# The first layer's router on rows that are not yet normalized

## What is computed

```
h = h + _L0_attn_ref(_layernorm(h, axis=-1), Wq, Wk, Wv, ...)
h = h + _L0_ffn_ref(_layernorm(h, axis=-1), expert_sel, keys, values)

def _L0_ffn_ref(x, expert_sel, keys, values):
    sel = jax.nn.sigmoid(xt @ expert_sel.T)
    sel_val, sel_idx = jax.lax.top_k(sel, TOP_K)          # TOP_K = 2 of E = 32
    w = zeros((T, E)).at[arange(T)[:, None], sel_idx].add(sel_val)
    h = jax.nn.relu(einsum('td,edh->teh', xt, keys))
    out = einsum('teh,te,ehv->tv', h, w, values)
```

## Time and profile before

| | us |
|---|---|
| median of 3 executions | 1150.5 |
| lowest, highest | 1148.85, 1151.22 |
| span of the profiled execution (first to last instruction) | 1146.4 |
| PE busy in the span | 936.4 (82%) |
| DVE busy | 876.0 (76%) |
| POOL busy | 673.3 (59%) |
| ACT busy | 511.0 (45%) |

### The profile page before, as it was taken

One profiled execution on the slowest core, in us unless ns is written; L12 is line 12 of the kernel. 1 busy time (PEld: TensorE's weight loads), 2 busy tenths in 40 slices (PEclk: granted clock), 3 DMA queues, 4 the chain that ended last, 5 costly groups with the idle time before them and its releaser, 6 DMA issues.

```text
span 1146.4 us, 21968 instructions
## 1 busy us (share of the span) xinstructions
PE 936.4 (82%) x6140; PEld 789.8 (69%) x6140; DVE 876.0 (76%) x3376; ACT 511.0 (45%) x1358; POOL 673.3 (59%) x622
## 2 busy tenths in 40 slices
PE   6999999999999973476667876566638999999992
PEld 2666676777667663466556765565638999999992
DVE  0588988988898966466678897677866888888883
ACT  1355555445555421111113545555524666656651
POOL 1036667666666633667777577766674545555552
PEclk9999999999999975678897887777759999999996
DMA  9856655666664032487789854455356888889886
GB/s 374 349 181 223 215 192 199 234 219 215 206 230 142 26 85 71 129 220 208 208 245 329 258 166 152 161 178 181 102 197 233 257 259 272 283 268 342 274 300 223
DMA packets 118667, 246.60 MB, mean 215 GB/s; under 512 B 20914, under 2 KB 85936, under 8 KB 112400
## 3 DMA queue, kind: packets, MB, share of 16 engines
q1 hardware_dynamic: 78016, 191.53, 50.6%
q0 software_dynamic: 18592, 34.68, 8.9%
q10 hardware_dynamic: 21936, 18.98, 5.5%
HBM read 201.68 MB, written 45.43 MB: 216 GB/s over the span
## 4 chain that ended last, share of the span: by engine, by line
PE 43%; DVE 22%; DMA 10%; issue 9%; SPq 7%; ACT 5%; POOL 3%; ACTq 1%; DVEq 0%; POOLq 0%
PE ps L950 11%; PE ps L931 9%; PE ps L734 4%; DMA x_hi<-results_L 3%; PE ps L801 3%; PE ps L785 3%; POOL lists_L L2061 2%; SPq L597 2%; SPq L599 2%; SPq L590 2%; DMA x_lo<-results_L 2%; PE ps L727 2%; PE ps L910 2%; PE ps L773 2%; PE ps L751 2%
## 5 line engine op out<-in xcount | busy, mean ns | idle before, releaser
L2061 POOL DMA_INDIRECT lists_L<-rows,slots x250 | 281.0, 1124 | 185.0 <-issue 173.1
L2089 POOL DMA_INDIRECT results_L<-xin x145 | 144.0, 993 | 122.7 <-DVE xin L1861 95.0
L2089 POOL DMA_INDIRECT results_L<-xin,place x146 | 143.8, 985 | 64.3 <-issue 39.5
L734 PE MATMUL ps<-xin,w_emb 128*128 128x512 f32 x292 | 138.2, 610 | 9.7 <-DMA w_emb<-in_w_main 8.6
L950 PE MATMUL ps<-xin,QK 128*128 128x128 f32 x838 | 115.3, 288 | 6.5 <-DVE QK L1813 4.4
L950 PEld LDWEIGHTS ps<-xin,QK 128*128 128x128 f32 x838 | 107.0, 203 | 8.0 <-DVE QK L1813 4.7
L931 PE MATMUL ps<-x_hi,x_lo 128*128 128x256 f32 (+1 forms) x324 | 98.5, 304 | 1.1 <-DVE x_lo L1829 1.1
L910 PE MATMUL ps<-ident,xin 128*128 128x128 f32 x291 | 65.9, 309 | 39.6 <-DMA xin<-lists_L 37.4
L2070 POOL TENSOR_TENSOR x_lo<-xin,x_hi 128x2048 fp32r<-128x2048 f32 x13 | 60.1, 4625 | 63.8 <-ACT x_hi L1118 63.5
L1271 ACT ACTIVATE QK<-ps,xin 128x256 f32<-128x256 f32 x164 | 64.4, 475 | 71.5 <-PE ps L931 71.5
L734 PEld LDWEIGHTS ps<-xin,w_emb 128*128 128x128 f32 x292 | 52.8, 194 | 59.2 <-issue 48.6
(11 more groups left out here) (310 smaller groups left out, 2443.1 us busy)
## 6 DMA issues: line engine op xcount, KB each, us to landing
xin<-in_x_main SPq DMA_DIRECT2D x48, 1536.0 KB, 6.8
xin<-in_w_L SPq DMA_DIRECT2D x81, 578.0 KB
xin<-in_w_L SPq DMA_DIRECT2D x98, 128.0 KB
xin<-lists_L SPq DMA_DIRECT2D x64, 132.0 KB
xin<-in_w_L ACTq DMA_DIRECT2D x65, 128.0 KB
xin<-in_difference SPq DMA_DIRECT2D x13, 640.0 KB
xin<-in_distance SPq DMA_DIRECT2D x13, 640.0 KB
x_hi<-results_L SPq DMA_DIRECT2D x11, 640.0 KB, 5.9
```

The source lines that it names most:

```text
L734: mm = pe.matmul(psE[h], w_emb[:, k, :], xin[h][c][:, n, :], start=(k == 0), stop=False, skip_group_check=True)
L2061: pool.indirect_dma_start(out=lists[l.name], out_offset=bass.IndirectOffsetOnAxis(ap=slots_of(l, g, h)[:, t, k:k + 1], axis=0), in_=buf[:, ...
L2089: pool.indirect_dma_start(out=results[l.name], out_offset=bass.IndirectOffsetOnAxis(ap=where, axis=0), in_=yblk[u][:, q, :], in_offset=Non ...
```

## The change

Only the first layer's routing is changed.

- The five transposes of the normalized rows on PE and ACT's copy of them are gone. The router multiplies `h1T` itself, which has its features along the partitions already, right after `b2`'s transposes of it, by `centered`: the router's matrix less each column's mean over the features. That matrix is made once at the start, by one product with ones (`sel_sums`) and one DVE instruction.
- The logits lie in the second pair of PSUM banks now. DVE copies them in `r2`, which is called right after the statistics of the group's rows, ahead of `a1_apply` (that makes `ntok`). The rest of the old `r2`, from the two largest on, is `r2_top` and stays where it was.
- The logits now lack the factor 1/sqrt(var + eps). A new DVE instruction, `scaled`, multiplies the two largest by it. ACT's exponential takes that product. `scaled` stands behind `r2_top`, directly ahead of `r2_gate`.
- In the last step (no attention left) DVE finds the two largest and the masks first, then refines the root and normalizes the rows, then makes the slots, and last the gates.
- Waits are added on PE for the logits' copy (ahead of the next product into the second pair) and for `htok`'s copy (ahead of the next product into the third pair).

The core of the diff. PE, the router's product (`r2`) and its place in `step`:

```diff
             def r2(l, g, h, j):
                 s = S[l.name]
-                pe.wait_ge(s.x2T_ready, g + 1)
+                if l is L1:
+                    pe.wait_ge(s.x2T_ready, g + 1)
+                else:
+                    pe.wait_ge(h1T_ready, g + 1)
+                    pe.wait_ge(consts_dve, 2)
                 for t in range(TILES):
-                    mm = pe.matmul(pair[2][0:l.rows, t * l.E:(t + 1) * l.E], x2T[l.name][:, t, :], selT[l.name][:, :],
-                                   start=True, stop=True)
+                    of_tile = x2T[:, t, :] if l is L1 else h1T[:, t * ROWS:(t + 1) * ROWS]
+                    mm = pe.matmul(logits[l.name][:, t * l.E:(t + 1) * l.E], of_tile,
+                                   selT["L1"] if l is L1 else centered[:, :], start=True, stop=True)
...
                 b2(g, h, j)
+                r2(L0, g, h, j)
                 tiles(4, 9)
...
                 if ahead_a:
                     a3(g + 1, o, jo)
-                r1(L0, g, h, j)
-                if ahead_a:
                     a4(g + 1, o, jo)
-                r2(L0, g, h, j)
```

ACT, the exponential (`r2`) and `front_step`:

```diff
                 if l is L0:
-                    act.activation(w.eg[:, :, :], w.top8[:, :, 0:TOP], ACT.Exp, scale=-1.0).then_inc(s.eg_ready, 1)
+                    act.activation(w.eg[:, :, :], w.eg[:, :, :], ACT.Exp, scale=-1.0).then_inc(s.eg_ready, 1)
...
                     a3(g + 1, o, jo)
-                r1_x2T(L0, g, h, j)
                 r1_rows1(L0, g, h, j)
```

DVE, the new function and `front_step`:

```diff
+            def scaled(g):
+                w = W["L0"]
+                dve.tensor_tensor(w.eg[:, :, :], w.top8[:, :, 0:TOP], LNB.rs[:, :, None].to_broadcast([ROWS, TILES, TOP]),
+                                  ALU.mult).then_inc(S["L0"].top_ready, 1)
...
                 r1(L0, g, h, j)
-                if ahead_a:
-                    a1_apply(g + 1, o, jo)
+                r2(L0, g, h, j)
+                if not ahead_a:
+                    st = r2_top(L0, g, h, j)
+                    r1_apply(L0, g, h, j)
+                    scaled(g)
+                    r3(L0, g, h, j, st)
+                    r3_slots(L0, g, h, j, st)
+                    r2_gate(L0, g, h, j, st)
+                    return
+                a1_apply(g + 1, o, jo)
                 r1_apply(L0, g, h, j)
...
-                st = r2(L0, g, h, j)
+                st = r2_top(L0, g, h, j)
+                scaled(g)
                 r2_gate(L0, g, h, j, st)
```

More of the change, by code:

```diff
@@ L291, in build @@
         pair = [ps[:, 2 + 2 * n:4 + 2 * n, :].rearrange("p b n -> p (b n)") for n in range(3)]
+        routed = {l.name: pair[2][0:l.rows, 0:TILES * l.E] for l in (L0, L1)}
+        logits = {"L0": pair[1][0:L0.rows, 0:TILES * L0.E], "L1": routed["L1"]}
+        sel_sums = pair[2][:, 2 * BANK - L0.E:]
         ident = sb("ident", [128, 128])
@@ L1477, in newton @@
                 dve.wait_ge(step, st.all())
-            NA, NBB, NR = 6, 1, {"L0": 11, "L1": 14}
+            NA, NBB = 6, 1
+            routing_steps = {l.name: Steps(0) for l in (L0, L1)}
             def e0(g, h, j):
@@ L1562, in r2 @@
                 s = S[l.name]
-                st = Steps(NR[l.name] * g + 3)
+                st = routing_steps[l.name]
                 E, w, p = l.E, W[l.name], l.rows
                 dve.wait_ge(s.lg_ps, g + 1)
-                logit = pair[2][0:p, 0:TILES * E].rearrange("p (t e) -> p t e", t=TILES)
+                logit = logits[l.name].rearrange("p (t e) -> p t e", t=TILES)
                 if l is L0:
-                    dve.tensor_copy(w.lg[:, :, 0:E], logit).then_inc(s.dveR, st.one())
+                    dve.tensor_copy(w.lg[:, :, 0:E], logit).then_inc(s.lg_read, 1)
                 else:
@@ L1571, in r2, with r2_top @@
                                                 rb_rows[:, None, :].to_broadcast([p, TILES, E]), ALU.add).then_inc(s.dveR, st.one())
-                dve.wait_ge(s.dveR, st.all())
+            def r2_top(l, g, h, j):
+                s = S[l.name]
+                st = routing_steps[l.name]
+                E, w, p = l.E, W[l.name], l.rows
+                if l is L0:
+                    dve.wait_ge(s.lg_read, g + 1)
+                else:
+                    dve.wait_ge(s.dveR, st.all())
                 dve.wait_ge(s.eg_ready, g)
@@ L1576, in r2 @@
                     ins = dve.max(w.top8[:, t, :], w.lg[:, t, 0:E])
-                if l is L0:
-                    ins.then_inc(s.top_ready, 1)
-                    dve.wait_ge(s.top_ready, g + 1)
-                else:
-                    ins.then_inc(s.dveR, st.one())
-                    dve.wait_ge(s.dveR, st.all())
+                ins.then_inc(s.dveR, st.one())
+                dve.wait_ge(s.dveR, st.all())
                 if l is L1:
@@ L1964, in chosen_first @@
             def chosen_first(g):
-                counts[g] = r2(L1, g, g % 2, g // 2)
+                r2(L1, g, g % 2, g // 2)
+                counts[g] = r2_top(L1, g, g % 2, g // 2)
             def slots_then(g):
```

47 lines of the change are left out of this document (27 added, 20 removed).

## The result

| | before | after |
|---|---|---|
| median of 11 executions on the same chip, us | 1148.9 | 1158.2 |
| span of the profiled execution, us | 1146.4 | 1154.1 |
| steps 2 to 11 of the front stage, pick to pick, us | 25.29 to 25.45 | 25.96 to 26.65 |
| PE busy in these ten steps, us | 248.5 of 253.4 | 249.3 of 263.5 |

The ratio is 1.0079 with a 95% interval of 1.0062 to 1.0097: 9.1 us slower, where 3.1 were forecast. The sign and the loop were right; the size was not. 1158.2 is just outside the range as it was written, 1148.0 to 1158.0. Counted from the kernel before it is further out: the range was set from a median of 1150.5 of three executions, so its upper end is 7.5 us slower, against the measured 9.1.

A forecast was written before the change was run, and what follows sets the result against it. The prediction took a loop through DVE's `x_lo`, POOL's held issue and `x_lo0`, and DVE's `oh` to bound the steps. Terms 8.8 - 0.5 - 0.7 - 4.5 = +3.1 us took 1150.5 to 1153.6 us, range 1148.0 to 1158.0.

The forecast's parts named there:

- What bounds the front stage in steps 0 to 12: Loop without slack: DVE's `x_lo`, POOL's held issue, two issues, `x_lo0`, DVE's `oh`, gate, `pick`, PE's L801, back to `x_lo`.
- Transposes and ACT's copy worth 0, product ahead of `ntok` worth 0: Ordinary steps, PE and ACT: removing 0.45 us of transposes gains nothing; the product's 0.9 us goes into slack at `oh`.
- The logits' copy, +0.23: DVE, ahead of `ntok`: the moved copy lies on the loop and costs 0.23 us a step, bounds 0.23 and 0.31.
- `scaled` and the round trip, +0.45: DVE behind `oh`: `scaled`, ACT's exponential and the steps between engines add 0.45 us a step, where slack is used up.
- The clock: Rival, 6%: PE's clock falls in the new gap ahead of the rank products or L801; +2 us a step, 1180.
- Steps 13 and 14: Last steps but one of the front stage: about -0.5 us in step 13 and -0.7 us in step 14.
- Step 15, -4.5: Last step: `top` starts 6.5 us earlier, `pick` and slots 5.0, the last send 4.5, and the rest moves along.
- that the lock is not the loop: Rival, 13%: the path through PE decides the steps, not POOL's hold on `oh`; +0.25 us a step, 1148.1.
- That `x_lo` does not hold POOL's issues: Rival, 12%: only the 0.45 us of the round trip is on the loop; +0.2 us in all, 1150.7.
- The one more issue: Rival, 5%: one more POOL issue starts before `x_lo` and drops out of the loop; 0 a step, 1144.8.
- A tail that gains nothing: Rival, 8%: the experts' stage does not start from the last send, so the 4.5 us are lost; +7.6, 1158.1.
- The start, 0: Kernel start: one product and one small DVE instruction stand where both engines wait for the first group; 0 us.

The follow-up runs named there:

- gate_on_act: Changed kernel, but ACT applies the logits' factor, so `scaled` and the round trip to ACT are gone: 1149.8 us, ratio 1.0011.
- copy_back: Changed kernel with the router's product and the logits' copy back at their old places in ordinary steps, `scaled` kept: 1154.4 us, ratio 1.0052.
- both: Changed kernel with the edits of `gate_on_act` and `copy_back` together: 1148.9 us, ratio 1.0000.
- before_short_low0: Kernel before with POOL's subtraction into `x_lo0` cut to a quarter in all steps but the first, part of the computation left out: 1140.7 us, ratio 0.9916.
- before_split: Kernel before with POOL's subtraction into `x_lo0` in four instructions instead of one: 1149.3 us, ratio 1.0018.
- best_split: `both` with PE's added `htok_ready` wait moved ahead of the other waits and POOL's subtraction in four instructions: 1150.4 us, ratio 1.0034.
- after_split: Changed kernel with POOL's subtraction into `x_lo0` in four instructions instead of one: 1161.0 us, ratio 1.0157.

## Why the prediction was right, and where its sizes were wrong

- **What bounds the front stage in steps 0 to 12**: right. The held issue, the two behind it, `x_lo0`, and `oh` 0.42 us behind its end stood in the changed kernel too. Cut, stretched and moved, POOL's subtraction moved the step each time.
- **Transposes and ACT's copy worth 0, product ahead of `ntok` worth 0**: right in this kernel. V's wait stayed at 0.49 us. The change as a whole is worth 1 us a step once `oh` is not held (23.8 against 24.8); its parts were not taken apart there.
- **The logits' copy, +0.23**: the row is right (0.21 from start to start), but the stretch from UH to `x_lo` grew only from 8.82 to 8.92 us, since one of the two normalizations of the step took 1.37 instead of 1.49. Between kernels it is 0.11 us. The term was twice too big; 12 steps of the difference, 1.4 us.
- **`scaled` and the round trip, +0.45**: 0.42 and 0.48 in the two comparisons (25.97 - 25.55, 25.92 - 25.44). Built from pieces of other rows, it held.
- **Forgotten**: the wait for `htok_ready` on PE, 0.12 us a step. I had read it in the diff as long fulfilled, and so as free. It made up for the error of the copy, so that a clean step, 25.97 us, agreed with 25.30 + 0.68 for partly wrong reasons.
- **The clock**, given 6% and a price of 2 us a step: this is the step that failed. It came true in five of twelve steps at 0.65 us each, 3.2 us of the 6.0 that the forecast missed, and in step 13. The prediction named a fall of the clock in the front stage, and more issues ahead of the held one, as signs of being wrong; both came. The argument against it, that PE is busy right ahead, did not hold. The price was too high, because the stretch at 1.2 GHz is short and the shift lets one more issue through. The case should have been priced as some falls inside the forecast, and not as a fall in every step.
- **Steps 13 and 14**, -0.5 and -0.7: +0.13 and -0.32. In step 14 the clock is lower from the start: V times Pr of that step takes 3.65 us in the changed kernel and 3.04 before. Step 14 is not a good measure, though: the kernel before and its three variants, which share it, have 27.06, 27.05, 25.53 and 25.49 us.
- **Step 15, -4.5**: right for the step. From V times Pr to the last group's send 459.23 - 437.02 = 22.2 us before, 466.42 - 449.00 = 17.4 after, -4.8. In these two profiles the stage behind it moved along, 687.2 and 687.7 us from the send to the end; with the scatter of that stretch (682.2 to 693.4) the agreement is partly luck, and the times say that some 4 us of the gain may be lost.
- **The rivals**: that the lock is not the loop (25.55 a step) fell with the clean step and with every edit of POOL's subtraction. That `x_lo` does not hold POOL's issues fell with the held row. The one more issue came only with a fall of the clock. A tail that gains nothing is not ruled out: step 15 itself is 4.9 us shorter, but the times do not show that gain.
- **The start, 0**: the edit costs nothing that shows, but this profile has 1.5 us there. The first pair's 24 matmuls took 12.26 instead of 10.57 us, at a mean clock of 0.87 instead of 1.00 between 18 and 31 us:

```profile
18.11 12.26 PE L741 MATMUL ps<-xin,w_emb 128*128 128x512 f32 x24 [2.23 <-DMA w_rest<-in_w_rest]
```

The wait for the load in front of them was 2.23 us there and 1.17 before. V of the first pair starts between 46.4 and 46.9 us in nine of the fourteen profiles, the kernel before among them, and between 48.1 and 48.8 in the other five: the changed kernel, `gate_on_act`, `copy_back`, `both` and `before_short_low0`, which has nothing of the change. So it is likely the run and not the kernel. How often the timed executions have it is open.

- **The rest of the miss**: of the 6.0 us, the falls are 3.2 and steps 13 and 14 are 1.0. What remains is in the main the balance of the start (+1.9 up to the first pick), the stretch behind the last send (+0.5), the difference between spans and medians (+1.4) and the long steps of the kernel before (-1.8). No run ties these to a term of the sum.

## What to carry over

When an engine stands in front of an instruction because another engine holds a resource, the time read as busy is a wait. In this kernel taking work off the engine that looks full gained nothing until that hold was shorter, and instructions between the hold and the end of the loop cost most or all of their length: find the hold, shorten it or start it earlier, and only then judge the rest. Count the waits that a diff adds behind the one that ends last, even if they are always fulfilled, and price a fall of the clock as something that can come in some steps when a gap of PE grows. Check a gain of one stage against the time of the whole: here 5.6 us in the profile's steps were 0 in the time.

## What was not expected of the hardware

- Four POOL subtractions in a row held DVE's `oh` until the last had ended in all steps of `before_split` and `best_split` (0.44 us behind 281.64), as one long one does. In six of twelve steps of `after_split` the first `oh` instruction got in ahead of the fourth piece and the second did not. Cutting the subtraction cost 0.41 us on POOL and gained nothing.
- A semaphore wait on PE that was long fulfilled costs 0.1 us behind the wait that ends last (0.79 against 0.68 us from `pick` to V times Pr), and nothing visible ahead of it (0.68).
- The granted clock fell to 1.2 GHz for some 3.5 us in the middle of a stage in which PE was busy for 95% (249.3 of 263.5 us), behind a gap of 0.8 us and 2 us of matmuls of 65 columns. In steps 1 to 11 of the kernels where that gap was about 0.37 us it did not. It also fell behind a wait of 1.5 to 1.6 us ahead of the rank products (`after_split` and `both`, step 12).
